# Clearing a spare tile on GpSimd behind every indirect fetch of the edge stage

## The reference

```python
h = (x_flat @ W_gat).reshape(M, HEADS, NUM_EXPERTS)     # 4 heads of 4 values for each node
a_src = (h * att_src).sum(-1)
a_dst = (h * att_dst).sum(-1)
e = leaky_relu(a_src[src] + a_dst[dst], negative_slope=0.2)
e_max = segment_max(e, dst, num_segments=M)
ee = exp(e - e_max[dst])
denom = segment_sum(ee, dst, num_segments=M)
msg = h[src] * (ee / (denom[dst] + 1e-16))[:, :, None]
agg = segment_sum(msg, dst, num_segments=M)
```

## Time and profile before

| | us |
|---|---|
| median of 3 runs | 6534.55 |
| lowest and highest run | 6527.07 and 6545.31 |
| the profiled execution | 6565.2 |
| its span | 6563.5 |
| TensorE busy | 5217.5 (79%) |
| VectorE busy | 4890.5 (75%) |
| ScalarE busy | 2537.8 (39%) |
| GpSimd busy | 2268.8 (35%) |

### The profile page before, as it was taken

How to read it: one execution, slowest core, us unless ns; L and a number is a source line. 1 busy time by engine, 2 the same in 40 slices (tenths; PEclk the granted TensorE clock), 3 DMA queues, 4 the chain that set the end, 5 groups by cost and what they waited for, 6 DMA issues and landing times. The chain is left out here.

```text
span 6563.5 us, 111024 instructions
## 1 busy us (share of the span) xinstructions
PE 5217.5 (79%) x41117; PEld 3540.3 (54%) x41184; DVE 4890.5 (75%) x8592; ACT 2537.8 (39%) x4432; POOL 2268.8 (35%) x2268
## 2 busy tenths in 40 slices
PE   6577968885469999971699999999994088967998
PEld 3462236554246666541577877778773025852452
DVE  6878988887878888870478888888886357767657
ACT  3443433333246666650233343333432043222332
POOL 0010010002223333325566666656663601014555
PEclk8778989997679999985799999999997598978999
DMA  0200000112210000001111121111111000030241
GB/s 17 78 6 1 20 23 29 35 41 65 72 32 6 6 9 11 10 10 40 22 39 40 37 41 41 41 36 41 40 40 27 8 1 3 3 65 15 68 105 33
DMA packets 241447, 206.47 MB, mean 31 GB/s; under 512 B 116682, under 2 KB 215923, under 8 KB 239251
## 3 DMA queue, kind: packets, MB, share of 16 engines
q1 hardware_dynamic: 173630, 147.27, 7.8%
q0 software_dynamic: 67408, 53.34, 5.3%
q10 hardware_dynamic: 12, 0.39, 0.0%
HBM read 113.55 MB, written 67.86 MB: 28 GB/s over the span
## 5 line engine op out<-in xcount | busy, mean ns | idle before, releaser
L3391 PE MATMUL edges_bank<-part_room,hot_room 128*128 128x512 f32 x7680 | 1778.8, 392 | 237.2 <-DVE hot_room L3482 190.0
L3391 PEld LDWEIGHTS edges_bank<-part_room,hot_room 128*128 128x128 f32 x7680 | 1440.3, 188 | 575.7 <-issue 253.6
L3373 POOL DMA_INDIRECT XT<-gat_node_table,edges_idx x1088 | 1113.8, 1024 | 706.4 <-issue 327.8
L3412 ACT COPY XT<-edges_bank 128x512 f32<-128x512 f32 x960 | 527.4, 605 | 1071.6 <-PE edges_bank L3391 695.3
L3500 DVE COPY_PREDICATED XT<-edges_tabs_p,XT 128x1280 f32<-128x1280 int32 (+3 forms) x768 | 648.3, 844 | 37.6 <-DVE edges_acc_s L3548 7.3
L3482 DVE TENSOR_SCALAR hot_room<-edges_lanes,edges_nodes 128x640 fp32r<-128x640 f16 x768 | 394.4, 576 | 298.8 <-PE edges_bank L3391 134.6
L1791 ACT ACTIVATE GT<-attc_sc,attc_nm 128x256 f32<-128x256 f32 x1024 | 399.8, 481 | 42.5 <-DVE attc_nm L1857 42.5
L1805 ACT ACTIVATE GT<-attc_sct 128x1024 f32<-128x1024 f32 x256 | 262.3, 1025 | 330.7 <-PE attc_sct L1725 329.7
L1856 DVE TENSOR_REDUCE attc_mx<-attc_sc 128x4 f32<-128x1024 f32 x256 | 313.3, 1224 | 89.3 <-PE attc_sc L1714 88.2
L1714 PE MATMUL attc_sc<-XT,attc_tT 64*128 64x256 f32 x2048 | 295.3, 407 | 52.5 <-ACT GT L1791 49.8
L505 POOL TENSOR_TENSOR X<-H,ln_f_mean 128x1024 f32<-128x1024 f32 x5 | 11.4, 2279 | 912.3 <-DVE ln_f_shift L542 912.3
(11 more groups left out here) (836 smaller groups left out, 10114.2 us busy)
## 6 DMA issues: line engine op xcount, KB each, us to landing
edges_lanes<-gat_places SPq DMA_DIRECT2D x192, 160.0 KB
gat_states<-GT SPq DMA_DIRECT2D x32, 768.0 KB
XT<-gat_node_table,edges_idx POOLq DMA_INDIRECT x1088
expert_pairs<-in_L_ffn_W_dram SPq DMA_DIRECT2D x48, 256.0 KB
XT<-XT SPq DMA_DIRECT2D x32, 256.0 KB
XT<-XT SPq DMA_DIRECT2D x64, 128.0 KB
XT<-XT SPq DMA_DIRECT2D x128, 64.0 KB
sorted_in<-stats SPq DMA_DIRECT2D x1, 5056.0 KB
```

The costliest lines, as they stand in the source:

```text
L3373: nc.gpsimd.indirect_dma_start(out=rows[:, k, c, :], out_offset=None, in_=q.t_table, in_offset=bass.IndirectOffsetOnAxis(ap=idx[:, k, c:c ...
L3391: m = nc.tensor.matmul(banks[t % BANKS][:], hot[:, (k * GROUPS + j) % 2, b, t, :], parts[:, p, b].rearrange("p u c -> p (u c)"), start=b = ...
L3412: nc.scalar.copy(fetched[:, (k * GROUPS + j) % 2, t].rearrange("p u c -> p (u c)"), banks[t % BANKS][:]).then_inc(fetched_in, 1)
```

## The change

Behind each of the 34 fetches of a chunk GpSimd clears a small tile `spacer` of 128 lanes by 256 bf16 words, which nothing reads. Ahead of each clear stands a wait for the clear before, since all write the same tile. One SBUF tile and one semaphore, which begins at 1, are added. The two chunks ahead of the loop get the clears too, so there are 32 x 34 = 1088 of them.

```diff
@@ -3073,6 +3073,7 @@
 PACE_BEHIND = 2 * PER_GROUP
+SPACER = 256
@@ -3276,7 +3277,7 @@
-        att = st.sb("att", [P, CH])
+        att, spacer = st.sb("att", [P, CH]), st.sb("spacer", [P, SPACER], BF16)
@@ -3305,6 +3306,7 @@
+        spaced = st.sem("spaced")
@@ -3364,6 +3366,8 @@
+                pool.sem_inc(spaced, 1)
+
                 def gather(n, k, banks_before):
                     pool.wait_ge(idx_ready, n + 1)
                     wait_apart(pool, rows_used, n + 1, passed)
@@ -3373,6 +3377,8 @@
                         nc.gpsimd.indirect_dma_start(
                             out=rows[:, k, c, :], out_offset=None, in_=q.t_table,
                             in_offset=bass.IndirectOffsetOnAxis(ap=idx[:, k, c:c + 1], axis=0)).then_inc(gathered[k], 16)
+                        wait_apart(pool, spaced, n * BY_DMA + c + 1, passed)
+                        nc.gpsimd.memset(spacer[:], 0.0).then_inc(spaced, 1)
```

## The result

The median of four runs went from 6534.47 us (6527.07 to 6545.31) to 6464.57 us (6456.34 to 6471.02): a ratio of 0.9895, 95% interval 0.9884 to 0.9907, **1.05% or 70 us faster**. The forecast was 6561, the range 6526 to 6665. The profiled execution took 6461.08 us, against 6565.2 before; 23 of these 104 us lie ahead of the edge stage, which the change does not touch (the stage's first matmul starts at 3151.1 and 3174.2), so what follows compares the stage alone.

What follows compares the result with a forecast made beforehand. TensorE was taken to set the edge stage's pace, GpSimd having 0.355 us room a fetch. The clear's 0.31 + 0.02 + 0.05 = 0.38 us exceeds it by 0.025, times 1054 = 26 us: 6561 us, range 6526 to 6665.

Steps and rivals of the forecast that it cites:

- the lower bound: Edge stage: the clear only adds work, so at most TensorE's idle time, about 50 us, could be won.
- GpSimd's pauses: GpSimd's waits on TensorE's columns in the edge stage, read as pacing that leaves it room for the clears.
- My sign of error: If the time moves while GpSimd still pauses for TensorE's columns, the predicted mechanism is wrong altogether.
- The clear: GpSimd's added clear behind each fetch: 0.31 us itself, plus 0.05 us for VectorE in the way.
- The gap: GpSimd's idle time around the clear: 0.02 us behind the fetch, and an unchanged 0.30 us before the next fetch.
- rival A: The clears fit GpSimd's room, as the next fetch starts up under the clear: 0.32 us added, 6535 to 6545; chance 0.38.
- The room: GpSimd's spare time in the edge stage: 1.682 us available for each of 1054 fetches against 1.327 used, leaving 0.355.
- 0.7 us a chunk: Delay of VectorE's comparisons by the clears in the edge stage; counted as nothing, with 5 us allowed.
- B: A fetch behind a clear starts 0.47 us late, as behind other elementwise work: +205 us, 6740; chance 0.07.
- C: The clear is half as long, as 128 words of 32 bits: 0.27 us added, no loss, 6536; chance 0.06.
- D: Faster: evenly spread fetches disturb VectorE's comparisons less, and with them TensorE's waits: 6510; chance 0.04.
- the range's upper end: Top of the forecast range: 0.48 us added a fetch, +132 us, given as 6665.

Runs made afterwards that it cites:

- e1: Kernel before the change, without GpSimd's waits on TensorE's finished columns; 7416.74 us, ratio to before 1.1338.
- e11: Kernel before the change, each indirect fetch replaced by GpSimd clears that keep it busy about as long; 6516.40 us, ratio to before 0.9953.
- e8: Changed kernel with clears of 384 elements a lane in place of 256; 6587.52 us, ratio to before 1.0073.
- e9: Kernel before, no clear; each fetch from a chunk's third on waits until the fetch two before it has landed; 6657.21 us, ratio to before 1.0168.
- e5: Changed kernel with four spare tiles in turn, each clear waiting for the one four before, without GpSimd's column waits; 6521.30 us, ratio to before 0.9968.

## Why the prediction was wrong

**The step that failed** is the lower bound: "the clear adds work and takes none off; what could be won is TensorE's idle time in the stage ... about 50 us". It took the distance between fetches for something that costs only GpSimd's own time. It has an effect on others: indirect fetches 1.25 us apart make TensorE's column counts late once a run has lasted some 5 to 9 us (kernel before), and slow TensorE's own issue when it goes on (after 14 us and more in e1). The clears set them 1.43 us apart, and that is worth 77 us of the stage. The rows were there to ask: 34.4 us of "issue" on TensorE, an idle time that nothing in the program explains, and 61.5 us of GpSimd's waits and 74.7 of VectorE's (the comparisons' row above) put down to a DMA that has nothing to do with them. The 50 us were also too small as a bound: busy time counts the 0.39 us of a matmul behind every stall, of which 0.16 otherwise lie under the next one. By starts it is 1826 - 1743 = 83.

**GpSimd's pauses** "<-PE edges_bank" were read as pacing, hence as room. Part of the 316 us was the late count itself, seen by GpSimd; in e11, where the count is never late, most of the pauses are of 1.06 us, one with each column. My sign of error, "if the time moves while GpSimd still pauses for columns", rested on the same reading; the pauses went and the time fell.

**The clear** was priced rightly: 0.31 + 0.05 for VectorE, measured 0.382 in the mean (0.33 alone, 0.56 for the 22% that meet a comparison; 23% were expected). By the rule that the prediction quoted from the Trainium skill ("SBUF — State Buffer", section "Who interferes with whom") it would have been, by the estimate there, 0.37; the rows do not tell the two apart.

**The gap** was wrong: 0.02 behind the fetch and 0.30 again ahead of the next. The next fetch begins 0.16 us behind the clear, which thus fills half of the old gap. An undisturbed pair takes 1.43 us, 0.18 more than a fetch before and not 0.33. That is the outcome of rival A, whose 0.32 us, with VectorE's share, compares with 0.38 + 0.16 - 0.30 = 0.24, and the reason that GpSimd fits: 1.61 us a fetch over the loop, at the 1.60 (54.4 / 34) that TensorE now needs. It fits barely: its last fetch starts 4.4 us ahead of the row that reads it, 23.6 before:

```profile
L3377 POOL DMA_INDIRECT XT<-gat_node_table,edges_idx x1088: 940/950/3200, 3143.2 to 4904.6; - x182
...
L3539 DVE TENSOR_TENSOR stats<-XT,edges_dst_p x32: 669/678/687, 3237.3 to 4909.0; 128x256 f32<-128x256 f32 x32
```

**The room** itself (each 0.01 us above it costs 10.5 us) was right as a mechanism, as e8 and e9 show, at another value: 1.60 and not 1.682, since TensorE's pace is no longer slowed.

**VectorE** was priced at 0.7 us a chunk; its comparisons took 65 ns more each, 1.6 us a chunk (24 x 0.065). It can have cost no more than the 7 us by which the stage is still above 1743, as VectorE now waits less for columns (70.7 us against 134.6).

**The rivals.** A had the right picture of GpSimd and the wrong time. B and C did not come. D had the sign, but by another road: "fetches spread more evenly could disturb VectorE's comparisons less", while they were disturbed more. Its chance of 0.04 came from the bound above. The sums hold, but for the range's upper end: 0.125 x 1054 more than 6534.55 is 6666 and not 6665, which changes nothing.

## What to carry to other kernels

Idle time that ends with "issue" on the engine that sets the pace, or with a DMA that cannot matter there, is a question to be answered before any sum is made; bursts of work that an engine sees at one moment (five copies at once) are its companion. A neighbour's instruction stream can cost more by its rhythm than by its busy time: indirect fetches that need not be early are better spaced out over the stage, close to the pace at which they are needed, and the spacing has a lower edge (here 1.43 us did it with one tile and not with four, 1.48 did it with four too) and an upper one (1.60 us a fetch, where they become the bound). A throttle that looks like slack may be what protects another engine, as e1 shows.

## What the runs showed of the hardware that was not expected

Indirect fetches of 128 rows, issued by GpSimd without a break, slow TensorE, with which they share no data and, in e1, no semaphore: in the kernel before ScalarE saw columns up to 8 us late in runs of them 1.25 us apart, and in e1's runs of 34 TensorE issued a matmul only every 1.4 to 2.8 us (725.7 us in the stage). With fetches 1.53 us apart, or with clears in their place, neither is seen. VectorE's signals to ScalarE stayed on time: in the kernel before, too, the scan's result is copied 0.03 us behind the scan's end in the mean of the chunks.

The Trainium skill ("SBUF — State Buffer", section "Who interferes with whom") says that "PE and ACT never wait on anyone" and that DMAs never contend with an engine. The rule is one of SBUF's ports. Read as "no DMA slows TensorE", it does not fit this case, and the measurement decides: e1's 725.7 us of "issue" are gone with clears between the fetches (e5, also without column waits), and with clears in their place none is left of the 34.4 (e11). Whether the delay lies at the ports, in the way of the semaphores, in that of TensorE's instructions or in the recording of the trace, no run here tells, and that stays open.
